# A decoder kernel: the transpose of the maxima's three parts, ahead of or behind the query and key projection

## The reference, cut to what matters

```python
# L0_ffn: inside the first layer's expert block, on RMS-normed rows
q, k = _rms(heads(wq), qn_w), _rms(heads(wk), kn_w)
attn = softmax(where(causal, q @ k.T * HD ** -0.5, -inf)) @ v

# L1_attn: low-rank projections
Q, K, V = (x @ W_dq) @ W_uq, (x @ W_dkv) @ W_uk, (x @ W_dkv) @ W_uv
out = softmax(where(causal, Q @ K.T / sqrt(16), -inf)) @ V

# L1_xattn: rotary positions, keys and values from the context, a band of 64
scores = q . k over the window; m = max(scores); e = exp(scores - m)
ctx = (e / sum(e)) @ v
```

## Time and profile before

| | us |
|---|---|
| median of 3 runs | 1427.04 |
| lowest, highest | 1426.36, 1427.63 |
| the profiled execution | 1428.32 |
| its span on the core | 1426.3 |
| PE busy in the span | 1361.6 (95%) |
| DVE, ACT, POOL busy | 732.8, 515.3, 286.3 |

### The profile page before, as it was taken

One profiled execution on the slowest core, in us unless ns is written; L12 is line 12 of the kernel. 1 busy time (PEld: TensorE's weight loads), 2 busy tenths in 40 slices (PEclk: granted clock), 3 DMA queues, 4 the chain that ended last, 5 costly groups with the idle time before them and its releaser, 6 DMA issues.

```text
span 1426.3 us, 30313 instructions
## 1 busy us (share of the span) xinstructions
PE 1361.6 (95%) x12024; PEld 955.1 (67%) x12024; DVE 732.8 (51%) x1762; ACT 515.3 (36%) x1004; POOL 286.3 (20%) x380
## 2 busy tenths in 40 slices
PE   6999999998999999889998999999999899999996
PEld 5888888885566666556664466575757677777764
DVE  5665555554566665367753122011112555678886
ACT  2212111221455555446654422122121444444444
POOL 2000000101111112388844000000000200124421
PEclk9999999998899999999999999999999999999999
DMA  6300000001222220012200100000000000000001
GB/s 205 62 13 0 1 1 1 1 1 35 46 48 63 53 59 24 2 43 74 62 17 10 56 0 0 0 1 0 0 0 0 3 3 4 13 17 16 16 6 53
DMA packets 35984, 36.04 MB, mean 25 GB/s; under 512 B 11696, under 2 KB 32544, under 8 KB 35856
## 3 DMA queue, kind: packets, MB, share of 16 engines
q1 hardware_dynamic: 35856, 34.23, 9.3%
HBM read 31.61 MB, written 1.86 MB: 23 GB/s over the span
## 4 chain that ended last, share of the span: by engine, by line
PE 67%; ACT 3%; DVE 2%; issue 2%; POOL 2%; DMA 0%; SPq 0%; DVEq 0%; ACTq 0%; POOLq 0%
PE banks L270 32%; PE banks L704 7%; PE banks L688 4%; PE banks L869 3%; PE banks L811 3%; PE banks L824 3%; PE banks L864 3%; PE banks L805 2%; PE banks L720 2%; PE banks L263 2%; ACT area L1248 2%; PE banks L852 2%; ACT area L1325 1%; POOL area L1109 1%; PE banks L762 1%
## 5 line engine op out<-in xcount | busy, mean ns | idle before, releaser
L1582 DVE TENSOR_REDUCE Y_room<-banks 112x2 f32<-112x750 f32 x128 | 115.5, 936 | 91.4 <-PE banks L688 91.4
L1658 DVE TENSOR_REDUCE area<-banks 112x8 f32<-112x896 f32 x96 | 100.2, 1086 | 76.6 <-PE banks L811 76.6
L1248 ACT ACTIVATE area<-banks,Y_room 125x896 f32<-125x896 f32 x96 | 96.7, 1007 | 95.3 <-PE banks L704 95.3
L1325 ACT ACTIVATE area<-banks 112x896 f32<-112x896 f32 x96 | 82.8, 914 | 121.1 <-PE banks L869 121.1
L270 PE MATMUL banks<-room,area 128*112 128x256 f32 (+1 forms) x384 | 118.3, 458 | 0.7 <-ACT area L1180 0.7
L1798 DVE SCALAR_TENSOR_TENSOR X<-banks,area,X 112x192 f32 (+1 forms) x64 | 26.5, 417 | 160.0 <-PE banks L270 160.0
L704 PE MATMUL banks<-room,area 64*125 64x224 f32 x768 | 102.6, 387 | 4.8 <-ACT area L1248 3.3
L1381 ACT ACTIVATE room<-banks 128x448 f32<-128x448 f32 x72 | 39.2, 544 | 183.3 <-PE banks L270 183.3
L270 PE MATMUL banks<-area,room 128*128 128x224 f32 x512 | 100.9, 359 | 2.0 <-ACT area L1200 2.0
L249 POOL TENSOR_TENSOR rstd<-mv,kcol 112x1 f32<-112x1 f32 x32 | 6.1, 192 | 469.1 <-DVE mv L1421 469.1
L270 PEld LDWEIGHTS banks<-area,room 128*128 128x128 f32 x512 | 98.1, 194 | 2.7 <-ACT area L1200 2.3
(11 more groups left out here) (233 smaller groups left out, 2497.0 us busy)
## 6 DMA issues: line engine op xcount, KB each, us to landing
Y_room<-in_ctx SPq DMA_DIRECT2D x16, 375.0 KB
area<-in_ctxT SPq DMA_DIRECT2D x64, 93.8 KB
l<-in_l SPq DMA_DIRECT2D x2, 1024.0 KB, 6.3
room<-in_ctxT SPq DMA_DIRECT2D x16, 112.0 KB, 2.2
out<-X SPq DMA_DIRECT2D x16, 112.0 KB, 1.9
X<-in_x SPq DMA_DIRECT2D x1, 1568.0 KB, 17.6
room<-in_Wq SPq DMA_DIRECT2D x1, 1024.0 KB, 5.0
room<-in_Wk SPq DMA_DIRECT2D x1, 1024.0 KB, 8.2
```

Of the source, the lines that this page charges most:

```text
L1248: a_.activation(b_pT[g][:, c, :, :], banks[0:KC, 4:6, 0:QN], ACT.Exp, bias=b_bias[v][:, c:c + 1]).then_inc(Bs["ex"].sem, 1)
L1325: a_.activation(c_pT[:, i * 8 * S:(i + 1) * 8 * S].rearrange("p (j n) -> p j n", j=2), banks[0:S, 2 + 2 * i:4 + 2 * i, 0:4 * S], ACT.Exp). ...
L1582: v_.tensor_reduce(b_nb[u][:, 4 * a + k:4 * a + k + H + 1:H], banks[0:S, 2 * a:2 * a + 2, 0:SC], AX_X, ALU.max, negate=True).then_inc(Bs[" ...
L1658: v_.tensor_reduce(c_nb[:, 8 * i:8 * i + 8].rearrange("q (j n) -> q j n", j=2), banks[0:S, 2 + 2 * i:4 + 2 * i, 0:4 * S].rearrange("q j (n ...
```

## The change

In a step, `project_qk(g + 3)` with its wait now comes ahead of the transpose of `c_n3`, and the transpose stands right ahead of the transposes of `c_o` and `c_h`. Nothing is added or removed; instructions of the other engines are in the same order as before.

```diff
                         last.then_inc(W["st"].sem, 1)
+                    if live(g + 3):
+                        if live(g - 3):
+                            pe.wait_ge(W["xu"].sem, W["xu"].at(g - 2))
+                        project_qk(g + 3)
                     if live(g):
                         pe.wait_ge(W["sp"].sem, W["sp"].at(4 * (g + 1)))
                         pe.wait_ge(W["ue"].sem, W["ue"].at(g - 1))
                         T3.transpose(pb[6][0:3 * H, 0:S], c_n3, ident[0:S, 0:S]).then_inc(W["nt"].sem, 1)
-                    if live(g + 3):
-                        if live(g - 3):
-                            pe.wait_ge(W["xu"].sem, W["xu"].at(g - 2))
-                        project_qk(g + 3)
                     if live(g - 2):
```

## The result

The changed kernel takes 1429.97 us, the median of 14 runs; the kernel before took 1427.10 over as many runs beside them. The ratio is 1.0025, with a 95% interval of 1.0017 to 1.0033, so the loss is 2.4 to 4.7 us: clear of no change, with the 0.2% that I had named inside the interval. I had forecast 1.9 us of loss and called it the same. The sign was right and the time lies in the range; the size was too small by about half.

The account below looks back on a forecast made before the run. PE was taken to bound L0_ffn and L1_xattn. Per step 0.09 + 0.10 - 0.115 = 0.07 us more, over 28 steps 1.9 us, onto 1427.04 gives 1428.9 us; range for 8 in 10: 1426.4 to 1430.6.

Parts of the forecast that it names:

- The bound: PE bounds L0_ffn and L1_xattn; in L1_attn PE waits for ACT's exponentials at the mask matmuls.
- First term: Right behind the 32-row tiles the projection's first weight load is not hidden: 0.09 us more a step.
- Second term: L876 between projection and L263 costs 0.10 us as one more transpose; its old place cost 0.115 us.
- The drain of the array: From the tiled products' start to whatever follows stays 0.96 us, as the array runs empty in either order.
- The steps counted: 12 steps of L0_ffn and 16 of L1_xattn pay 0.07 us each, 1.9 us in all.
- L1_attn at 0: Steps 16 to 28 add 0, since L805 waits 0.25 us for ACT anyway; without that cover 0.9 us.
- Step 0 at 0: The projection fits into PE's wait, L263 starts 0.8 us earlier, but later transposes wait for POOL's chain: gain 0.
- ACT, SP, DVE: Engines behind the moved transpose: L1330 near 655.0, L1335 at most 0.1 us later, SP's write 0.4 later; all at 0.
- the sum against the median: The steps' 1.9 us go onto the runs' median of 1427.04 us, giving 1428.9 us.
- one fall only, behind the gap in step 1: Rival: clock falls to 1.2 GHz between 622 and 626 us, 1.2 us more, 1430.1 in all; chance 0.15.
- The rival that the order makes no difference: The exposed load is compensated or hidden, a step 0.02 us cheaper to 0.03 dearer: 1427.0 us; chance 0.17.
- a saved change of kind: Rival: two fewer switches between matmul and transpose per step save 0.1 us in 28 steps: 1424.2 us; chance 0.06.

Follow-up runs that it names:

- The three single kernels: The change in steps 1 to 12, 17 to 28 or 29 to 44 alone, against the kernel before: 1429.26, 1427.11 and 1426.08 us.
- e2: The change in the fill steps 0 and 16 alone, against the kernel before: 1425.85 us, ratio 0.9996.
- r_before: Old order with useless matmuls filling PE's waits in fills, drain and start of the experts, against the kernel before: 1424.19 us, ratio 0.9981.
- r_after: Changed order with useless matmuls in the fills, the drain and the start of the experts, against the kernel before: 1425.61 us, ratio 0.9999.

## Why the prediction was right or wrong

**The bound** was read rightly: PE in L0_ffn and L1_xattn, ACT's exponentials in L1_attn. The three single kernels have just their own steps longer, and L1_attn none.

**First term, the exposed load, 0.09 us:** right, 1.11 us for two 512-column records behind the tiles, and in L1_xattn 0.96 us from start to start for the first four of 256 columns (1305.73 to 1306.69), where it was 0.87 (1303.06 to 1303.93). Rows behind 64-row and 18-row tiles were good stand-ins for 32-row ones. **Second term, 0.10 against 0.115:** right. **The drain of the array, 0.96 us whatever follows:** right (653.32 to 654.27 in step 4, 0.956 before rounding).

**The steps counted, 28 at 0.07:** right, 0.81 + 1.08 us. **L1_attn at 0:** right, the wait paid. **Step 0 at 0:** right, and shown by e2; the 0.8 us came back as a wait for POOL's power, with 1.78 us where I had said 1.8. **ACT, SP, DVE:** right in that no full step is longer than the two terms make it; ACT's wait is 0.24 us and not 0.4.

**The step that failed is the sum against the median.** It put the difference of the steps onto the median with the clock as it was, so a change of the clock stood in it at nothing. I had it at full speed in the steps of the earlier trace rows and carried that over to all that follows them, and weighed one fall only, behind the gap in step 1, where no trace of the changed kernel has one: the PE was busy 1.64 us from 620.66 to 624.08, as the rival had worked out, and the clock stayed at 2.4 GHz up to 627.49. A fall elsewhere is a real rival; its price of 1.2 us was taken from another stretch, and that the fall in the drain costs 1.27 is luck. Luck too is that the measured time lies in the range, whose upper end was drawn for a fall in the wrong place. The drain of L0_ffn, with its waits of 1.67 and 1.50 us, begins where I had cut off the stretch of the earlier trace rows, at step 13; the trace of before showed them, and I had not weighed them. What the runs show in place of the nothing is 1.8 us over the step costs, with a mean clock of 0.9845 where before has 0.9854; a shift of 0.76 us in the old order brings as much. The traces leave room for it between step 13 and step 17, in the drain, the experts and the fill of L1_attn. How the 1.8 us divide among the falls there, and what sets them, stays open. I had given a fall of the clock 0.15.

The rival that the order makes no difference is out, and so is that of a saved change of kind: the full steps grew by 0.067 us each, and r_before and r_after differ by the step costs, not in its favour. Of the page "TensorE: Matmul & The Clock Gate" of the Trainium skill, the rule of the section "LDWEIGHTS (loading the stationary operand)" on the time of a load by columns had the right sign. The sentence of its section "The mechanism" by which a load overlaps running matmuls only where the row group differs is contradicted again: L880's load starts at 655.65 in step 4, beside the projection's last full-height record, and L880 costs 0.10 us.

## What to carry to other kernels

Behind a group of small tiles the first weight load is bare, so the narrowest weight should stand there; a weight of 112 columns cost 0.09 us each time. A small delay of a PE-bound stage cost two to three times itself here, where waits of the PE of 1 to 2 us follow, so look at each such wait of the whole program, take several traces, and fill the waits with matmuls before two orders are weighed against each other.

## What the runs showed of the hardware

The clock fell or held behind stretches that look alike. In before the PE was busy 1.75 us in the 3.42 us ahead of 755.46 and the clock stayed at 2.4 GHz; in the changed kernel it was busy 1.75 in the 3.42 ahead of 757.27 and the clock fell. Busy PE, before and changed kernel:

```profile
752.04:755.46 3.42, 1.75 (x39) 1.00 0.03 8
```

```profile
753.85:757.27 3.42, 1.75 (x39) 1.00 0.01 3
```

With still less, 1.64 us in the 3.42 ahead of 624.08 in the changed kernel, it stayed at 2.4 GHz. So this view does not tell on which side a stretch falls. The two of 1.75 us are not filled alike: transposes (L880, L263) take the first 0.27 us of the changed kernel's and the first 0.10 of that of before, and tiled and full-height matmuls nearly all the rest. Whether that matters was not tested, and what decides stays open. I had also not expected that the fall near 756 us would be there in all five traces with a longer L0_ffn and in one of five without, the drain being the same work.
